# GroupNorm and self-attention in fp32 on one core: loads, folds and first softmax of the first image in another order

## What is computed

```
xn  = groupnorm(x)            # 32 groups of 8 channels, over all tokens of the image
q, k, v = xn Wq + bq, xn Wk + bk, xn Wv + bv
p   = softmax(q k^T / 16)     # 1024 x 1024
out = x + (p v) Wo + bo
```

## Time and profile before

| | us |
|---|---|
| median of 3 runs | 1859.79 (1859.34 to 1862.06) |
| the profiled execution | 1862.75 |
| its span | 1861.1 |
| TensorE busy | 1833.9 |
| VectorE busy | 1642.1 |
| ScalarE busy | 981.8 |
| GpSimd busy | 94.0 |

### The profile page before, as it was taken

The page is one execution under the profiler, slowest core; times in us unless marked ns, Lnnn a source line. Parts: engine busy times, 40 slices in busy tenths (PEclk is TensorE's granted clock), DMA queues, the critical chain, the costliest instruction groups (busy, mean ns, idle before and its releaser), DMA issues.

```text
span 1861.1 us, 33031 instructions
## 1 busy us (share of the span) xinstructions
PE 1833.9 (99%) x11690; PEld 1670.2 (90%) x11690; DVE 1642.1 (88%) x2793; ACT 981.8 (53%) x1347; POOL 94.0 (5%) x109
## 2 busy tenths in 40 slices
PE   8899999999999999999999999999999999999997
PEld 7799998998998998989999989989889999899896
DVE  5898998988988989989889889889899898898885
ACT  3545545546546455456455465465564554654652
POOL 0000000000000000000000000000000000000000
PEclk9899999999999999999999999999999999999998
DMA  3211212202222112222122222132221122220211
GB/s 113 57 44 36 68 56 68 68 19 60 68 56 68 55 24 68 56 68 68 32 47 68 56 68 62 17 68 60 64 68 36 42 68 56 68 67 12 67 23 24
DMA packets 29296, 101.92 MB, mean 55 GB/s; under 512 B 3681, under 2 KB 4706, under 8 KB 29282
## 3 DMA queue, kind: packets, MB, share of 16 engines
q0 software_dynamic: 9216, 33.56, 11.6%
q1 hardware_dynamic: 20066, 68.17, 11.2%
HBM read 68.16 MB, written 67.11 MB: 73 GB/s over the span
## 4 chain that ended last, share of the span: by engine, by line
PE 98%; DVE 1%; ACT 0%; DMA 0%; issue 0%; SPq 0%; POOLq 0%
PE ps_s L593 48%; PE ps_o L681 13%; PE ps_o L679 13%; PE ps_o L680 13%; PE ps_o L593 10%; DMA s_buf<-in_L_conv_bq_dram 0%; ACT p_hi L314 0%; ACT s_buf L320 0%; DVE s_buf L465 0%; DVE p_lo L473 0%; PE ps_o L605 0%; DVE s_buf L490 0%; DVE query_max L452 0%; PE ps_s L605 0%; SPq L213 0%
## 5 line engine op out<-in xcount | busy, mean ns | idle before, releaser
L679 PE MATMUL ps_o<-v_hi,p_hi 128*128 128x258 f32 x2048 | 580.5, 283 | 3.2 <-DVE p_lo L473 3.2
L681 PE MATMUL ps_o<-v_hi,p_lo 128*128 128x258 f32 x2048 | 582.0, 284 | 0.0
L680 PE MATMUL ps_o<-v_lo,p_hi 128*128 128x256 f32 x2048 | 578.1, 282 | 0.0
L314 ACT ACTIVATE p_hi<-s_buf 128x1024 fp32r<-128x1024 f32 x256 | 272.1, 1063 | 527.2 <-DVE s_buf L465 527.2
L593 PE MATMUL ps_s<-g_hi,h_hi 128*128 128x512 f32 x1024 | 406.3, 397 | 7.5 <-ACT s_buf L306 7.5
L593 PE MATMUL ps_s<-g_hi,h_lo 128*128 128x512 f32 x1024 | 400.8, 391 | 0.0
L593 PE MATMUL ps_s<-g_lo,h_hi 128*128 128x512 f32 x1024 | 399.6, 390 | 0.0
L679 PEld LDWEIGHTS ps_o<-v_hi,p_hi 128*128 128x128 f32 x2048 | 387.5, 189 | 6.1 <-issue 2.2
L680 PEld LDWEIGHTS ps_o<-v_lo,p_hi 128*128 128x128 f32 x2048 | 389.7, 190 | 2.8
L306 ACT ACTIVATE s_buf<-ps_s 128x512 f32<-128x512 f32 x512 | 293.6, 608 | 185.5 <-PE ps_s L593 182.8
L681 PEld LDWEIGHTS ps_o<-v_hi,p_lo 128*128 128x128 f32 x2048 | 388.5, 190 | 0.0
(11 more groups left out here) (86 smaller groups left out, 2213.4 us busy)
## 6 DMA issues: line engine op xcount, KB each, us to landing
x_t<-in_x_turned_dram SPq DMA_DIRECT2D x64, 512.0 KB, 4.0
out_dram<-in_x_dram SPq DMA_DIRECT2D x64, 512.0 KB, 7.6
out_dram<-o_buf POOLq DMA_DIRECT2D x64, 512.0 KB, 5.4
s_buf<-in_L_conv_Wq_dram SPq DMA_DIRECT2D x1, 256.0 KB, 3.1
s_buf<-in_L_conv_Wk_dram SPq DMA_DIRECT2D x1, 256.0 KB, 3.1
s_buf<-in_L_conv_Wv_dram SPq DMA_DIRECT2D x1, 256.0 KB
s_buf<-in_L_conv_Wo_dram SPq DMA_DIRECT2D x1, 256.0 KB
s_buf<-in_L_conv_bq_dram SPq DMA_DIRECT2D x1, 1.0 KB, 4.0
```

What stands on the lines that cost most here:

```text
L314: nc.scalar.activation(p_hi[c][:, rows, :], s_buf[c][:, rows, :], ACT.Exp, scale=SCALE).then_inc(p_hi_done, 1)
L679: nc.tensor.matmul(ps[:, 0:VC], p_hi[c][:, m, cols], v_hi[:, m, :], start=m == 0, stop=False)
L680: nc.tensor.matmul(ps[:, 0:C], p_hi[c][:, m, cols], v_lo[:, m, :], start=False, stop=False)
L681: last = nc.tensor.matmul(ps[:, 0:VC], p_lo[c][:, m, cols], v_hi[:, m, :], start=False, stop=m == T - 1)
```

## The change

- SyncE loads the turned x of image 0 first, then Wq, Wk, bq and the rest as before.
- The three turned weights are evicted by ScalarE instead of VectorE. ScalarE's order in the prologue is: turned Wq, turned Wk, first half of `h_hi`, `a_hi`, second half of `h_hi`, turned Wv.
- TensorE: mean and variance of image 0 stand right behind the two turned weights, ahead of the first fold. The second fold and `out_bias` go behind the scores of chunk 0, and TensorE waits behind them for `vo_lo`. `ps_vo` and `ps_ob` are now the banks `ps_o[2]` and `ps_o[3]`.
- VectorE: `fold_rest` of the first fold stands between the two `h_rest`; `g_rest` comes ahead of the copies of bv. The second `fold_rest` and `out_bias` stand in the first softmax.
- The first softmax of image 0 has its own order on ScalarE and VectorE (`first_softmax`). On ScalarE the parts of v and the evictions of chunk 1 stand between the exponentials. On VectorE the statistics of image 1 (`channel_stats(1)`, `channel_sums(1)`) move from ahead of the row maxima to the end of the softmax.
- The mean and variance matmuls of image 1 move from among the scores of chunk 1 to behind `attend(0, 0, 0)` and `attend(0, 0, 1)`.

Images 1 to 31 are the same but for this. The diff, cut to its core:

```diff
--- before.py
+++ after.py
...
-        ps_a, ps_vo, ps_gb, ps_ob = ps_s[0], ps_s[1], ps_s[3], ps_stat[1]
+        ps_a, ps_vo, ps_gb, ps_ob = ps_s[0], ps_o[2], ps_s[3], ps_o[3]
...
+            load_turned(0)
             load_weight(0, wq, wqk_in)
             load_weight(1, wk, wqk_in)
             with nc.allow_non_contiguous_dma(reason="a short vector, once"):
                 sp.dma_start(bq_col, bq.rearrange("(k p) -> p k", p=P)).then_inc(wqk_in, 16)
-            load_turned(0)
             load_weight(2, wv, wvo_in)
             load_weight(3, wo, wvo_in)
             with nc.allow_non_contiguous_dma(reason="a short vector, once"):
...
-            def h_parts(b):
-                after(act, s_ps, b * 16)
-                for k in range(K):
-                    act.wait_ge(h_done, b * 2 + (k + 1))
-                    nc.scalar.activation(h_hi[:, k, :], x_t[:, k, :], ACT.Copy).then_inc(h_hi_done, 1)
+            def h_part(b, k):
+                if k == 0:
+                    after(act, s_ps, b * 16)
+                act.wait_ge(h_done, b * 2 + (k + 1))
+                nc.scalar.activation(h_hi[:, k, :], x_t[:, k, :], ACT.Copy).then_inc(h_hi_done, 1)
...
-            act.wait_ge(fold_ps, 1)
-            nc.scalar.activation(a_hi[:], ps_a[:].rearrange("p (k n) -> p k n", k=K), ACT.Copy).then_inc(fold_hi, 1)
-            h_parts(0)
-            act.wait_ge(fold_ps, 3)
-            nc.scalar.activation(vo_hi[:], ps_vo[:].rearrange("p (k n) -> p k n", k=K), ACT.Copy).then_inc(fold_hi, 1)
+            def turned_out(n):
+                act.wait_ge(w_turned_ps, n + 1)
+                nc.scalar.activation(turned[:, n, :, :], ps_turn[n][:].rearrange("p (k n) -> p k n", k=K),
+                                     ACT.Copy).then_inc(w_turned, 1)
+
+            def fold_first(n, hi, ps, value):
+                act.wait_ge(fold_ps, value)
+                nc.scalar.activation(hi[:], ps[:].rearrange("p (k n) -> p k n", k=K), ACT.Copy).then_inc(fold_hi, 1)
+
+            turned_out(0)
+            turned_out(1)
+            h_part(0, 0)
+            fold_first(0, a_hi, ps_a, 1)
+            h_part(0, 1)
+            turned_out(2)
             act.wait_ge(fold_done, 2)
             for i in range(4):
                 g_part(0, i)
...
+            def first_softmax():
+
+                fold_first(1, vo_hi, ps_vo, 3)
+                exponentials_hi(0, 0, 0)
+                exponentials(0, 0, 0)
+                v_part(0, 0)
+                v_part(0, 1)
+                exponentials_hi(0, 0, 1)
+                v_part(0, 2)
+                exponentials(0, 0, 1)
+                v_part(0, 3)
+                scores_out(0, 1, 0)
+                scores_out(0, 1, 1)
+                exponentials_hi(0, 0, 2)
+                exponentials(0, 0, 2)
+                scores_out(0, 1, 2)
+                scores_out(0, 1, 3)
+                last_exponentials(0, 0)
+                for m in range(4, T):
+                    scores_out(0, 1, m)
+
             def body(b, first, last):

                 scores_out(b, 0, 0)
@@ -354,15 +385,16 @@
                 for m in range(1, T):
                     scores_out(b, 0, m)
                 if first:
-                    for i in range(4):
-                        v_part(b, i)
-                softmax_beside(b, 0, nothing if first else (lambda i: v_part(b, i)))
-                scores_out(b, 1, 0)
-                last_exponentials(b, 0)
-                for m in range(1, T):
-                    scores_out(b, 1, m)
+                    first_softmax()
+                else:
+                    softmax_beside(b, 0, lambda i: v_part(b, i))
+                    scores_out(b, 1, 0)
+                    last_exponentials(b, 0)
+                    for m in range(1, T):
+                        scores_out(b, 1, m)
                 if not last:
-                    h_parts(b + 1)
+                    for k in range(K):
+                        h_part(b + 1, k)
                 softmax_beside(b, 1, nothing if last else (lambda i: g_part(b + 1, i)))
...
-            def turned_out(n):
-                dve.wait_ge(w_turned_ps, n + 1)
-                nc.vector.tensor_copy(turned[:, n, :, :],
-                                      ps_turn[n][:].rearrange("p (k n) -> p k n", k=K)).then_inc(w_turned, 1)
...
-            turned_out(0)
-            turned_out(1)
             channel_stats(0)
             dve.wait_ge(bn_done, 4)
             channel_sums(0)
+            group_spread(0)
+            group_variance(0)
+            normalise(0)
+            h_rest(0, 0)
             fold_rest(0, a_hi, a_lo, ps_a)
+            h_rest(0, 1)
             dve.wait_ge(fold_ps, 2)
             nc.vector.tensor_copy(g_bias[:], ps_gb[:, 0:K]).then_inc(fold_done, 1)
-            group_spread(0)
-            turned_out(2)
-            group_variance(0)
+            for i in range(4):
+                g_rest(0, i)
             dve.wait_ge(wvo_in, 16 * 4)
             dve.wait_ge(const_step, 9)
             for j in range(K):
                 nc.vector.tensor_scalar(bv_wide[:, j, :], ones[:], bv_col[:, j:j + 1], None, ALU.mult).then_inc(bv_ready, 1)
-            normalise(0)
-            for k in range(K):
-                h_rest(0, k)
-            fold_rest(1, vo_hi, vo_lo, ps_vo)
-            dve.wait_ge(fold_ps, 4)
-            nc.vector.tensor_copy(out_bias[:], ps_ob[:, 0:C]).then_inc(fold_done, 1)
-            for i in range(4):
-                g_rest(0, i)
+
+            def first_softmax():
+
+                part_maxima(0, 0)
+                query_maxima(0, 0)
+                row_maxima(0, 0)
+                fold_rest(1, vo_hi, vo_lo, ps_vo)
+                difference(0, 0, 0)
+                dve.wait_ge(fold_ps, 4)
+                nc.vector.tensor_copy(out_bias[:], ps_ob[:, 0:C]).then_inc(fold_done, 1)
+                difference(0, 0, 1)
+                difference(0, 0, 2)
+                v_rest(0, 0)
+                v_rest(0, 1)
+                p_rest(0, 0, 0)
+                v_rest(0, 2)
+                difference(0, 0, 3)
+                v_rest(0, 3)
+                p_rest(0, 0, 1)
+                p_rest(0, 0, 2)
+                channel_stats(1)
+                p_rest(0, 0, 3)
+                dve.wait_ge(bn_done, 8)
+                channel_sums(1)
...
                 if first:
-
-                    next_stats()
-                    for i in range(4):
-                        v_rest(b, i)
-                    channel_sums(b + 1)
-                    softmax_beside(b, 0, nothing, nothing, nothing, nothing, nothing)
+                    first_softmax()
...
             turn_weight(0)
             turn_weight(1)

+            mean_of_groups(0)
+            variance_of_groups(0)
             pe.wait_ge(w_turned, 2)
             fold(ps_a, wq_t, wk_t)

             for k in range(K):
                 product(ps_gb[:, k:k + 1], [(wk_t[:, j, k * P:(k + 1) * P], bq_col[:, j:j + 1]) for j in range(K)],
                         fold_ps if k == K - 1 else None)
-            mean_of_groups(0)
             pe.wait_ge(wvo_in, 16 * 4)
             turn_weight(2)
-            variance_of_groups(0)
-
+            pe.wait_ge(fold_done, 2)
             pe.wait_ge(w_turned, 3)
-            fold(ps_vo, wv_t, wo_sb)
-
-            pe.wait_ge(bv_ready, K)
-            pe.wait_ge(var_done, 1)
-            product(ps_ob[:, 0:C], [(bv_wide[:, j, :], wo_sb[:, j, :]) for j in range(K)]
-                    + [(ones[0:1, :], bo_row)], fold_ps)
-            pe.wait_ge(fold_done, 2)
             project_g(0)
-            pe.wait_ge(fold_done, 4)
+
+            def second_fold():
+                fold(ps_vo, wv_t, wo_sb)
+                pe.wait_ge(bv_ready, K)
+                product(ps_ob[:, 0:C], [(bv_wide[:, j, :], wo_sb[:, j, :]) for j in range(K)]
+                        + [(ones[0:1, :], bo_row)], fold_ps)
+                pe.wait_ge(fold_done, 3)

             def body(b, first, last):
                 for m in range(T):
                     scores(b, 0, m)
-                if not first:
+                if first:
+                    second_fold()
+                else:
                     for j in range(TQ):
                         attend(b - 1, 1, j)
                 project_v(b)
                 for m in range(T):
                     scores(b, 1, m)
-                    if m == (3 if first else 1) and not last:
+                    if m == 1 and not first and not last:
                         mean_of_groups(b + 1)
-                    if m == 5 and not last:
+                    if m == 5 and not first and not last:
                         variance_of_groups(b + 1)
                 for j in range(TQ):
                     attend(b, 0, j, last)
+                    if first and j == 0:
+                        mean_of_groups(1)
+                    if first and j == 1:
+                        variance_of_groups(1)
                 if not last:
                     project_g(b + 1)
```

## The result

| | us | ratio to before, 95% interval |
|---|---|---|
| before, median of 6 runs | 1860.94 (1859.34 to 1862.46) | |
| after, median of 6 runs | 1868.2 (1866.67 to 1869.07) | 1.0039 (1.0027 to 1.0051) |
| after, the profiled execution | 1866.67, its span 1865.1 | |

The prediction was +7.5 us and 1867.3. The hole among the scores of chunk 1 is gone; the time comes back in the first `project_g` of the next image.

What follows compares the result with a forecast made beforehand. TensorE was taken as the bound (98% of the last-ending chain), so only its idle or slow-clock time counted. project_g(1) 5.4 us late plus a 2.1 restart gave +7.5 on 1859.8: 1867.3, range 1863.0 to 1870.0.

Steps and rivals of the forecast that it cites:

- the deciding term: Image 1's mean, queued behind attend(0, 0, 0), delays h_lo; project_g(1) starts 5.4 us late, 7.5 with the restart.
- From the attention on: Attention start to project_g(1): mean after 3.3 us, then 15.0 to h_lo, TensorE waiting 6.3, restart 2.1.
- the pause: In project_g(1), TensorE waits 6.3 us for h_lo of image 1.
- the restart: Half-clock stretch behind idle time: 2.1 us at project_g(1) and at project_g(0), 2.7 at project_v.
- Loads: Kernel start: x ahead of the weights delays them by 2.65 us, so TensorE starts at 8.6 (bounds 1.6 to 3.5).
- Prologue: TensorE's steps from 8.6 sum to 10.95 us, so project_g(0) starts at 19.55 instead of 22.09.
- the first fold does not raise the clock: Prologue: fold with bias leaves TensorE at 1.2 GHz, so project_g(0) starts slow, costing 2.1 us (bounds 0 and 2.7).
- project_v: Behind chunk 0's scores: waits for vo_lo, starts at 44.7 after 0.5 to 3.5 us idle, with a 2.7 us restart.
- The sum: Whole kernel: project_g(1) 5.4 us late plus 2.1 restart, +7.5 us on median 1859.8, giving 1867.3.
- rival (a): Clock stays up over the pause ahead of project_v: attention from 61.4, +4.8 us, 1864.6; chance 0.23.
- (b): Clock up also at project_g(0), besides project_v: attention from 59.3, +2.7 us, 1862.5; chance 0.12.
- (c): project_g(1) does not wait, VectorE's way from mean to h_lo hidden behind the attends: -1.0 to -5.8 us; chance 0.05.

Runs made afterwards that it cites:

- e8_mean_late: Kernel before, with only the mean and variance matmuls of image 1 moved behind attend(0, 0, 0) and attend(0, 0, 1): 1869.71 us against 1861.31, ratio 1.0046.
- e1_mean_first: Changed kernel with the mean matmul of image 1 ahead of attend(0, 0, 0) and the variance behind it: 1863.24 us against 1860.68, ratio 1.0011.
- e2_stats_early: Changed kernel, image 1's channel statistics ahead of the first maxima, mean among chunk 1's scores, variance ahead of attend(0, 0, 0): 1860.35 us against 1860.68, ratio 0.9998.
- e5_all: Changed kernel with image 1's statistics, mean and variance beside chunk 0's scores, normalise and vo_lo earlier, v parts ahead of exponentials: 1855.16 us against 1860.6, ratio 0.997.
- e3_x_behind: Changed kernel with the loads in the old order, weights then x: 1868.04 us against 1860.68, ratio 1.004.
- e4_evict_only: Kernel before, ScalarE evicting chunk 1's first four score tiles ahead of the exponentials, image 1's variance matmul behind attend(0, 0, 0): 1860.94 us against 1860.68, ratio 1.0002.
- second measurement: The changed kernel itself, unedited, run again beside the experiments as their control: 1865.29 us against 1860.6, ratio 1.0029.
- e9_filled_twice: Changed kernel with TensorE's waits filled by unread matmuls, 12 ahead of project_v and 26 ahead of project_g(1): 1863.9 us against 1861.31, ratio 1.0013.
- e7_filled: Changed kernel with TensorE's wait for h_lo of image 1 filled by 26 unread matmuls: 1865.28 us against 1860.6, ratio 1.0026.
- e6_vo_early: Changed kernel with vo_lo ahead of the row maximum on VectorE: 1863.43 us against 1860.6, ratio 1.0015.

## Why the prediction was right

- **What bounds.** The prediction read image 0 as the only place where time moves, and the deciding term as the mean of image 1 queued behind `attend(0, 0, 0)`. e8_mean_late shows that term alone at +8.4 us; e1_mean_first, e2_stats_early and e5_all take it back in steps (the latter two together with other moves).
- **From the attention on** each number held: the mean read 3.2 us behind the start of the attention (3.3 predicted), 14.8 from there to h_lo (15.0), the pause 6.0 (6.3), the restart 2.3 (2.1).
- **Loads.** TensorE starts at 8.95 (8.6), between 7.9 and 8.95 in eight traces with x first and between 5.4 and 6.0 in five with the weights first. The means of the two are 2.7 us apart; priced were 2.65. e3_x_behind shows that taking this back does not take back the loss.
- **Prologue.** `project_g(0)` started at 19.18 (19.55). The step "the first fold does not raise the clock" failed: it rose near the end of the fold, and fell again behind the pause for g_bias (below). The restart was priced at 2.1 and measured 1.6, so the sum held for another reason than the one given. The start that it was compared with, 22.09, also belongs to the profiled execution alone: with the same prologue e4_evict_only and e8_mean_late have the clock up near the end of the first fold and start at 20.24 and 20.01, so the new order won about 1 us there and not 2.5.
- **project_v** started at 43.62 (44.7) with a pause of 3.0 (0.5 to 3.5) and the predicted restart, but that cost 1.6 and not 2.7. The price was too high for this execution only: behind the same pause of 3.0 us it was 2.9 in e1_mean_first (8.55 us) and 2.6 in e2_stats_early (8.25). With the earlier start this put the attention at 61.8 instead of 64.1, and `project_g(1)` at +2.8 instead of +5.4.
- **The sum.** In the profiled pair the stretch up to the scores of image 1 is +5.1 us, against +7.5 forecast; the start of `project_v` and its restart, 1.1 us each, are nearly all of the difference. That the medians give +7.3 all the same in the first measurement is luck: the sum started from an execution of before that was some 2 us slow in its prologue, and this made up for the two terms. The second measurement gives +4.7. So the side and the size hold, and 7.5 stands at the upper end of what was measured; that 1867.3 lay 0.9 from 1868.2 says little of the single terms.
- **Rivals.** No run is rival (a) or (b) as written, with the clock up ahead of `project_v`, or there and at `project_g(0)`, and down at `project_g(1)`. e9_filled_twice keeps the clock up at `project_v` and at `project_g(1)`; by the terms of the sum that is 7.5 - 2.7 - 2.1 = +2.7, and +2.5 was measured. (c), that only the earlier attention would count, is what e2_stats_early and e5_all get once the mean is early.

## What to carry to other kernels

Before an idle stretch of the busiest engine is removed, look at what the other engines do in it: here VectorE was busy for 7.36 of 7.54 us, so the pause only moved. A tiny matmul that another engine's long chain starts from must not stand behind a long tile in an in-order queue; what it costs is the tile plus the wait, and it is cheapest to do it where that other engine is idle anyway. Each new pause of TensorE of 3 us and more was followed here by a stretch at half clock that cost 1.5 to 2.9 us (thirteen such stretches in nine traces, ahead of `project_v` or `project_g(1)`, each against the same work at full clock), so it should be charged with a range of that size. And a single profiled execution should be placed among the timed ones before a time is compared with it.

## What the runs showed of the clock

The page of the profile shows a grant of 1.00 up to the first event of the clock, whatever the clock is. Weight loads tell it: groups of weight loads of the changed kernel at 15 to 16 us and at 16.3 to 17.1 (busy us, mean ns),

```profile
L633 PEld LDWEIGHTS ps_s<-s_buf 128*128 128x128 f32 x4 | 1.3, 337 | 0.4
```

```profile
L633 PEld LDWEIGHTS ps_s<-s_buf 128*128 128x128 f32 x7 | 1.2, 246 | 0.1
```

337 ns is about the duration at 1.2 GHz (333 in the earlier trace rows), and 246 is a mean over the two levels. So the clock rose at about 16.5 us, near the end of the first fold. In the profiled execution of before the fold left it down. That differs between executions too: in e4_evict_only, with the same prologue as before, a load of this shape takes 192 ns at 13 to 14 us, where before had 333:

```profile
L603 PEld LDWEIGHTS ps_s<-s_buf 128*128 128x128 f32 x2 | 0.3, 192 | 0.0
```

The first matmuls of `project_g(0)` of the changed kernel ran at full pitch, and then, without a new pause, at half:

```profile
19.95 0.57 PE L633 MATMUL ps_o<-h_hi,a_hi 128*128 128x512 f32 x1
20.32 0.63 PE L633 MATMUL ps_o<-h_lo,a_hi 128*128 128x512 f32 x1
```

```profile
20.50:23.00 2.50, 2.50 (x8) 1.91 (x7) 0.75 (x1) 0.69 (x1) 0.00 (x0) 0.50 0.99 372
```

I had not expected that the clock can fall after a pause of 1.5 us (17.7 to 19.18), nor that the fall can come 0.8 us after the work has gone on. It is the last pause before the fall, but no run isolates it as the cause. The eight traces with x first show all cases at that point. In two (e2_stats_early, e5_all; pause 1.3 us) the clock was up and stayed up. In three (the changed kernel, its control, e7_filled; 1.45 to 1.7 us) it was up or falling at the start and then down. In e1_mean_first (1.7 us) it had risen in the fold, with loads of 192 ns, and was down at the start (0.77 us for the first matmul). In e6_vo_early and e9_filled_twice it had not risen in the fold at all (loads of 333 ns). And in e4_evict_only it stayed up over 1.81 us. So what a short pause costs differs from execution to execution, and belongs into a range, not into a sum.
